# A transformer block on one core: narrow P blocks summed and masked on VectorE, row maxima turned by a DMA, variances from squares on ScalarE

## The reference

```python
mask = tril(ones((T, T))) * (arange(T) % 4 != 3)     # causal, and every fourth key is never seen
q, k, v = heads(x @ Wq + bq), heads(x @ Wk + bk), heads(x @ Wv + bv)
att = softmax(where(mask == 0, -inf, q @ k.T / sqrt(32)))
attention(x) = concat(att @ v) @ Wp + bp
idx = argmax(log_softmax(logits) + gumbel(u))
ffn(x) = x @ W[idx] + b[idx]
x = x + layernorm(attention(layernorm(x)))
x = x + layernorm(ffn(layernorm(x)))
```

## Time and profile before

| | |
|---|---|
| median of the runs | 2315.77 us |
| span of the profiled execution, first to last instruction (the page has no other time for it) | 2314.4 us |
| TensorE busy | 2226.8 us, 96% |
| VectorE busy | 1712.2 us, 74% |
| GpSimd busy | 1703.5 us, 74% |
| ScalarE busy | 1558.7 us, 67% |
| time of the busiest DMA queue's packets, as a share of 16 engines' span | 23.5% |

### The profile page before, as it was taken

How to read it: one execution, slowest core, us unless ns; L and a number is a source line. 1 busy time by engine, 2 the same in 40 slices (tenths; PEclk the granted TensorE clock), 3 DMA queues, 4 the chain that set the end, 5 groups by cost and what they waited for, 6 DMA issues and landing times.

```text
span 2314.4 us, 42414 instructions
## 1 busy us (share of the span) xinstructions
PE 2226.8 (96%) x14484; PEld 932.2 (40%) x14484; DVE 1712.2 (74%) x4758; ACT 1558.7 (67%) x2822; POOL 1703.5 (74%) x1563
## 2 busy tenths in 40 slices
PE   4899999999999999999999999999999999999997
PEld 2444433433444443343344444343344444334322
DVE  7978776876477878687368878778728787768876
ACT  7657667677755767667864766767776576675673
POOL 3248699789735879978962769988983486997852
PEclk9999999999999999999999999999999999999998
DMA  7213122112233213112132413111124231211101
GB/s 214 69 35 89 36 56 64 36 29 82 55 93 75 59 41 70 39 35 59 48 92 59 100 31 80 45 34 43 45 60 103 68 78 34 60 46 49 27 1 37
DMA packets 222818, 137.42 MB, mean 59 GB/s; under 512 B 145194, under 2 KB 195082, under 8 KB 222602
## 3 DMA queue, kind: packets, MB, share of 16 engines
q1 hardware_dynamic: 222310, 134.65, 23.5%
q10 hardware_dynamic: 292, 0.07, 0.0%
HBM read 39.69 MB, written 16.78 MB: 24 GB/s over the span
## 4 chain that ended last, share of the span: by engine, by line
PE 74%; DVE 9%; issue 6%; POOL 5%; ACT 4%; DMA 2%; SPq 0%; POOLq 0%; ACTq 0%; DVEq 0%
PE acc L1310 13%; PE acc L1346 13%; PE acc L1330 12%; PE acc L1281 9%; PE acc L1282 9%; PE acc L1283 9%; PE acc L1361 5%; POOL P L845 3%; ACT P L960 3%; DVE MP L1065 2%; PE acc L1334 2%; DVE acc L1061 2%; DVE STA L1016 1%; PE acc L1286 1%; PE acc L1318 1%
## 5 line engine op out<-in xcount | busy, mean ns | idle before, releaser
L960 ACT ACTIVATE P<-acc,EX 128x512 f32<-128x512 f32 (+2 forms) x1920 | 1084.5, 637 | 421.8 <-PE acc L1330 204.0
L845 POOL TENSOR_TENSOR P<-P 128x512 f32<-128x512 f32 x982 | 1219.4, 1277 | 65.1 <-PE acc L1346 51.3
L1065 DVE TENSOR_REDUCE MP<-acc 128x1 f32<-128x512 f32 (+1 forms) x1088 | 718.4, 679 | 172.2 <-PE acc L1310 169.4
L1310 PE MATMUL acc<-KST,QST 96*128 96x512 f16 (+10 forms) x2112 | 596.0, 334 | 24.7 <-DVE MP L1065 8.1
L1330 PE MATMUL acc<-QST,KST 98*128 98x512 f16 (+2 forms) x1920 | 589.2, 355 | 13.5 <-ACT P L960 6.6
L1061 DVE CUSTOM_DVE_ANT_0 acc<-acc,CB 128x96 f32<-128x96 f32 (+7 forms) x1024 | 450.3, 455 | 189.0 <-PE acc L1310 186.6
L1346 PE MATMUL acc<-P,V 128*32 128x512 f32 (+2 forms) x3840 | 430.6, 545 | 1.4 <-ACT P L960 0.9
L1310 PEld LDWEIGHTS acc<-KST,QST 96*128 96x128 f16 x2112 | 192.8, 97 | 364.7 <-issue 62.6
L1330 PEld LDWEIGHTS acc<-QST,KST 98*128 98x128 f16 x1920 | 183.2, 97 | 280.5 <-ACT P L960 69.5
L824 POOL TENSOR_TENSOR RR<-RR,NHALF 128x1 f32<-128x1 f32 x256 | 140.9, 555 | 185.8 <-DVE RR L1022 105.0
L836 POOL TENSOR_TENSOR QKL<-SC,QKH 128x384 f16<-128x384 f32 (+1 forms) x128 | 134.3, 1049 | 123.5 <-ACT QKH L935 123.4
(11 more groups left out here) (152 smaller groups left out, 2506.2 us busy)
## 6 DMA issues: line engine op xcount, KB each, us to landing
QST<-QKH SPq DMA_DIRECT2D x128, 128.0 KB, 3.2
XR<-in_L_attn_x_dram SPq DMA_DIRECT2D x60, 256.0 KB, 2.9
out_dram<-XR SPq DMA_DIRECT2D x60, 256.0 KB, 2.2
KST<-QKH SPq DMA_DIRECT2D x128, 96.0 KB, 2.6
XB<-in_L_attn_x_dram SPq DMA_DIRECT2D x48, 252.0 KB
QST<-QKL SPq DMA_DIRECT2D x64, 128.0 KB, 3.3
KST<-QKL SPq DMA_DIRECT2D x64, 96.0 KB, 2.7
XB<-in_L_attn_x_dram SPq DMA_DIRECT2D x20, 256.0 KB, 3.2
```

The lines of the kernel that those rows point to most:

```text
L845: e.tensor_tensor(P[:, acc, a, :], P[:, acc, a, :], P[:, buf, a, :], ALU.add).then_inc(g_s, 1)
L960: e.activation(P[:, p_buf[u, g, sb_], a, t0:512], bank(*step)[:, t0:512], ACT.Exp, scale=EX[:, 1:2]).then_inc(a_e, 1)
L1065: e.tensor_reduce(maxima(u, g)[:, r, a, ci:ci + 1], bank(*s)[:, 0:n], AX.X, ALU.max).then_inc(v_m, 1)
L1310: i = e.matmul(bank(*s)[:, 0:n], QST[0:96, h, 128 * r:128 * r + 128], KST[0:96, h, c0:c0 + n], start=True, stop=True)
```

## The change

1. **Mask.** The matmul that adds the mask to the scores is gone. VectorE takes the minimum of P and a mask of 0 and 1e38 after the exp, one instruction for the 4 x 176 elements of a block's four heads. pv, sum and add of such a block wait for it.
2. **Narrow blocks.** In 63 of 64 windows the two narrow blocks are added to the accumulator by VectorE (four heads in one instruction) and not summed on TensorE. The accumulator's own sum now comes last. In unit j = 0 block 0, summed directly before, is the accumulator of these two adds.
3. **Pairs.** GpSimd adds two heads with one instruction.
4. **Maxima.** MHL is padded to 128 columns and turned by a transposing DMA from SyncE's queue. TensorE's four transposes and ScalarE's copy are gone; the following DMAs to QST wait for the landing.
5. **Variances.** For the norms after the two projections (k = 1 and 3) ScalarE squares the row with an accumulated sum, and one small VectorE instruction stands where BN_STATS, BN_AGGR and a tensor_scalar stood. For the first norm of all units but the first, the four powers on GpSimd are one instruction.
6. **Exp.** The scale of the exp is in a register, where it was a [128, 1] operand.
7. **Planner.** The durations are changed to fit, and with them every engine's list.

```diff
+    MASK, NARROW, SQUARE, BATCH, QUADS = True, True, True, True, 2
+    EXP = 0.833, 93
+    def narrow_added(self, u, g):
+        return self.NARROW and not (u == self.NU - 1 and g == 3)
+    def added(self, u, g):
+        j = u % self.NJ
+        whole = [s for s in range(1, 3 * j + 1) if not self.on_pe(u, g, s)]
+        return whole + [3 * j + 1, 3 * j + 2] * self.narrow_added(u, g)
+    def adders(self, u, g, sb):
+        j = u % self.NJ
+        if sb > 3 * j:
+            return [("dve", 0, 4)]
...
+        return [("gp", a, self.QUADS) for a in range(0, 4, self.QUADS)]
...
-            add("pe", s - 0.2, 300, ("shift", u, g), [("dve", "peaks", u, g)])
-            add("act", s - 0.2, 480, ("shift", u, g), [("pe", "shift", u, g)], [("MROW", ("sp", "shift", u, g))])
+            add("sp", s - 0.2, 1250, ("turn_m", u, g), [("dve", "peaks", u, g)], [("MROW", ("sp", "shift", u, g))])
...
+                if masked and self.MASK:
+                    add("dve", at, 830, ("mask", u, g, sb), exps)
+                    exps = [("dve", "mask", u, g, sb)]
...
+                    e.dma_start_transpose(MROW[:, :].rearrange("p (o n) -> p o n", o=1), MHL[:, n % 2, :]).then_inc(d_h, 16)
...
+                    e.tensor_tensor(P[:, acc, h, :], P[:, acc, h, :], P[:, buf, h, :], ALU.add).then_inc(g_s, 1)
...
+                    e.activation(VOID[:, :], bank("proj", job, 0), ACT.Square, accum_out=SQ[:, k // 2, r:r + 1]).then_inc(a_s, 1)
...
                     e.activation(P[:, p_buf[u, g, sb_], a, t0:512], bank(*step)[:, t0:512], ACT.Exp,
-                                 scale=EX[:, 1:2]).then_inc(a_e, 1)
+                                 scale=factor).then_inc(a_e, 1)
...
+                        e.scalar_tensor_tensor(out=RR[:, k, 0, r:r + 1], in0=SQ[:, k // 2, r:r + 1], scalar=1.0 / 512,
+                                               in1=EC[:, k // 2:k // 2 + 1], op0=ALU.mult, op1=ALU.add).then_inc(v_ln, 1)
...
+                elif kind == "mask":
+                    part = P[:, p_buf[u, g, sb_], :, T0[i]:T0[i] + MW]
+                    for a in range(4):
+                        dv.wait_ge(a_e, AC["exp", u, g, sb_, a])
+                    e.tensor_tensor(part, part, MASKT[i].rearrange("p (o n) -> p o n", o=1).broadcast_to([128, 4, MW]),
+                                    ALU.min).then_inc(v_k, 1)
...
+                    e.tensor_tensor(P[:, acc, h, t0:512], P[:, acc, h, t0:512], P[:, buf, h, t0:512], ALU.add).then_inc(v_s, 1)
...
-                        pe.wait_ge(d_cb, 16)
-                        i = e.matmul(bank(*s)[:, t0:t0 + MW], IDB, MASKT[dg], start=False, stop=True)
```

More of the change, by code:

```diff
@@ L21, in most_chunks, with width @@
     return max(len(chunks(384 * j + 96 * (r + 1))) for r in range(4))
[L24 to L31, removed]
+def width(j, sb):
+    return (512, 512, 344, 176)[max(sb - 3 * j + 1, 0)]
 def p_blocks(NB, NJ):
@@ L278, in attend @@
                     [] if sb else [("psO", ("dve", "out", u, g))])
-            before = []
[L280 to L284, removed]
-                add("pe", s + place / (last + 1) + 0.02, 1.65 * w + 60, ("sum", u, g, sb), done + before,
+                if sb in self.added(u, g):
+                    i = self.added(u, g).index(sb)
+                    for who, a0, n in self.adders(u, g, sb):
+                        before = [("pe", "pv", u, g, 0)]
+                        if masked and self.MASK and not j:
+                            before.append(("dve", "mask", u, g, 0))
+                        if i:
+                            was = self.added(u, g)[i - 1]
+                            before = [(self.adder_on(u, g, was, a), *self.adder(u, g, was, a)) for a in range(a0, a0 + n)]
+                        done = [("dve", "mask", u, g, sb)] if masked and self.MASK else [("act", "exp", u, g, sb, a) for a in range(a0, a0 + n)]
+                        add(who, at, 142 + 2.12 * n * w if who == "gp" else 100 + 1.04 * n * w, ("add", u, g, sb, a0), done + before)
@@ new lines, in attend @@
+            before = []
+            for sb in blocks:
+                w = 512 if sb == "acc" else width(j, sb)
+                if sb == "acc":
+                    was = self.added(u, g)[-1]
+                    done = [(self.adder_on(u, g, was, a), *self.adder(u, g, was, a)) for a in range(4)]
+                    at = 3 * j if 3 * j + 1 in blocks else last
+                else:
+                    done = [("dve", "mask", u, g, sb)] if sb >= 3 * j and self.MASK else [("act", "exp", u, g, sb, a) for a in range(4)]
+                    at = sb
+                add("pe", s + at / (last + 1) + 0.02, 1.65 * w + 60, ("sum", u, g, sb), done + before,
@@ L294, in attend @@
-            add("dve", s + 0.95, 1600, ("invert", u, g), [("pe", "sum", u, g, last)]
+            add("dve", s + 0.95, 1600, ("invert", u, g), before
                 + [("dve", "out", *divmod(s - 1, 4))] * (s > 0))
@@ L707, in valued @@
             return max(AC["evac", ("v", u, a)] for a in range(3))
-        def exped(u, g, sb_):
-            return max(AC["exp", u, g, sb_, a] for a in range(4))
         block = ctx.enter_context(nc.Block())
```

294 lines of the change are left out of this document (171 added, 123 removed).

## The result

The changed kernel takes 2492.74 us (median of 4 runs, 2483.91 to 2504.35), the kernel before 2316.39 beside it. The ratio is 1.077, 95% interval 1.073 to 1.080: slower by 7.7%. The forecast was 2237 us and faster, its range ended at 2330.

What follows compares the result with a forecast made beforehand. TensorE was taken as the bound: 2314.4 - 138 = 2176 us, plus 60 us lost with a nearly full VectorE, made 2236 us of span and a forecast of 2237 us; the 8-in-10 range was 2165 to 2330.

Steps and rivals of the forecast that it cites:

- what leaves TensorE: On TensorE: masking matmuls 59 us, transposes 20 us and narrow sums 59 us go, together 138 us.
- VectorE's own work: On VectorE: 1712 us less 140 of statistics, plus 22 of tiny steps and 310 of masks and adds, 1904 us.
- the waits: On VectorE: 318 masks and narrow adds held up by GpSimd's adds, 200 us in all, bounds 0 to 380.
- The long narrow adds: A sign on VectorE: adds of 1376 elements would take above 2 us each.
- I take two and a half times that loss, 3% of some 2000 us: 60 us: TensorE's added loss from sharing fixed lists with a nearly full VectorE: 60 us, bounds 0 to 120.
- TensorE's own 2177: The run time if TensorE kept its present idle time: 2176 us of span plus 1.4 us.
- TensorE alone: Rival, 22%: TensorE stays alone at the bound, VectorE's waits are absorbed, 2177 us.
- VectorE is the bound: Rival, 15%: with waits of 380 us VectorE has 2284 us of work, and the kernel takes 2290 us.
- The end of each window: Rival, 18%: VectorE's chain adds 5.0 us at each window's end; from 2.2 us uncovered the kernel is slower.
- SyncE's part: On SyncE's queue: transposing DMAs bring a window's maxima 2.3 us later, costed at nothing; uncovered, 147 us.
- its price by mean residual, 245 us: On VectorE: by the skill's rule alone a meeting with a GpSimd pair costs 1.1 us, the waits 245 us.

Runs made afterwards that it cites:

- e5: The changed kernel with GpSimd's adds of two heads working on 16 of 512 columns, same lists and waits: 2281.38 us, ratio 0.985.
- e7: The changed kernel with GpSimd adding one head per instruction, as before the change, lists planned anew: 2516.60 us, ratio 1.087.
- f1: The changed kernel, same lists, with 16-column one-SBUF-input maxima replacing masks and narrow adds, and the one-column step as a tensor_scalar: 2253.74 us, ratio 0.973.
- f2: The kernel before the change with GpSimd's adds working on 16 of 512 columns, same lists: 2301.98 us, ratio 0.993.
- e6: The changed kernel, same lists, with masks and narrow adds cut to 16 columns a head, still two SBUF inputs: 2354.91 us, ratio 1.017.
- e2: The changed kernel with the mask put on the scores by TensorE again, lists planned anew: 2367.00 us, ratio 1.022.
- e3: The changed kernel with the narrow blocks summed by TensorE again, the mask staying on VectorE: 2436.44 us, ratio 1.051.
- e4: The changed kernel with mask and narrow sums on TensorE again and the one-column step as a tensor_scalar: 2296.58 us, ratio 0.992; repeated, 2294.78 us, ratio 0.990.
- e9: The changed kernel with the mask's table in PSUM, seven banks for the planner, narrow sums on TensorE, one-column step as a tensor_scalar: 2340.92 us, ratio 1.011.
- e10: The same as e9, with the same lists, but the mask's table read from SBUF: 2485.76 us, ratio 1.074.
- f3: e4 with the 126 narrow adds on GpSimd, four heads to an instruction: 2273.32 us, ratio 0.981.
- e11: The changed kernel with the mask on GpSimd as a 0/1 product, narrow sums on TensorE, one-column step as a tensor_scalar: 2300.75 us, ratio 0.993.
- e1: The changed kernel with the one-column step as a tensor_scalar with one SBUF input, same lists: 2483.22 us, ratio 1.072.

## Why the prediction was wrong

**Right: what leaves TensorE, and VectorE's own work.** I had 1904 us for VectorE without meetings; e5, nearly without them, shows 1901.9. Masks were 0.84 us in the working and are 0.875 at the shortest; adds of 1376 elements were 1.52 and are 1.58 at several places of the timeline.

**Right in sum, wrong in kind: the waits.** I took 200 us, and VectorE is busy 2105.2 us, where I had 2104. But I made it 318 chances of a wait of 0.9 us, less than half of the instruction in the way, and set the upper bound at 1.2. The trace has 192 masks with a median of 1.07 us and a maximum of 7.23, and a single column that stood for 11.98. The evidence I had, one add of 1.16 us, came from a place where VectorE got its turn after one GpSimd instruction. I generalized the mean from that, and e7 shows that the length of that instruction isn't what counts. I also missed one class of meeting: the 128 one-column steps, which I priced at 0.174 us by a row of the same operation. That row had one input in PSUM; the new step has both in SBUF. By the difference to e5 the waits are 118 us at the masks (302.2 against 183.8), 67 at the one-column steps (90.6 against 23.7) and 17 at the narrow adds (192.2 against 175.1). The steps that I had priced for waits have 136 of my 200, and steps that I had given none have the rest: that 2105 met 2104 is luck. The long narrow adds took 1.74 us on the mean, where I wanted over 2 as a sign.

**The step that failed** is in the sum: "I take two and a half times that loss, 3% of some 2000 us: 60 us". What stood there was 316 us, 197 of them from the meetings (below). I had read the 3% from a stretch in which GpSimd was 93% busy, whose lateness TensorE hardly felt (2.3 us of 200). VectorE stands twice in TensorE's way: its masks and narrow adds come before pv and the sums, and its reductions empty the banks of the peaks. No other work can pass a stalled instruction, because the lists are fixed; from 604 us on one such stall held TensorE for 10.04 us. TensorE's idle time was 276 us and not 147, and 108 of the added 188 us stand before pv and the sums. And I left the clock out: 0.955 against the 0.991 of before.

Of the 316 us between TensorE's own 2177 and 2493 I had forecast 60. By the runs they are:

| | us | what it holds |
|---|---|---|
| my 2176 + 1.4 | 2177 | TensorE with before's idle time, an estimate |
| f1 | 2254 | and the new places of the steps, nearly no length, no meeting |
| e5 + 15 (what short adds on GpSimd gave in f2) | 2296 | and the length, nearly no meeting |
| changed kernel | 2493 | and the meetings |

So the meetings cost some 197 us, the length 42, and 77 are for the new places together with whatever else my 2177 had wrong (TensorE's waits for rows from MROW are 16 us in f1, and 0.3 before). The split holds only in this order: with short steps, e6 against f1, nearly the same waits cost 101 us. Without meetings the change would by this estimate have brought 0.9%, and not 3.4%. That the mask is the larger part, e2 and e3 show: taking it away gives 126 us although TensorE gets some 59 us of matmuls back, for the narrow adds it is 56 us.

**The rivals.** "TensorE alone" is refuted by f1 as well. "VectorE is the bound" had the right culprit with the wrong picture: VectorE was idle for 379 us. "The end of each window", the slower one, came nearest. It named the direction, the instructions and the place where most of the added idle time stands: 69.4 + 42.1 us before pv and the sums, or 1.7 us in each of 64 windows, where it asked for 2 or more. What it had too small is the waits, 2.7 of the 5.9 us of its chain. In e5 that chain has its full length and nearly no meetings, and TensorE waits only 18.9 + 9.5 us there; the other 83 us came with the meetings. The planner, the transposing DMAs, ScalarE's squares and the pairs are cleared by e4, at least without the new steps on VectorE beside them. SyncE's part holds nearly: TensorE waited 10.6 us for rows from MROW.

The Trainium skill, "SBUF — State Buffer", section "Who interferes with whom", gave the mechanism, and e9 against e10 bears it out. I gave it no rival of its own, because its price by mean residual, 245 us, looked like mine. By its words the second waits until the first is finished; here the wait outlasted five GpSimd instructions and more.

## What to carry to other kernels

Before an elementwise step is put on VectorE, count its inputs in SBUF: with two of them beside a GpSimd that works through long runs, the price can be not the step's length but the rest of the run, and everything behind it in the list pays. One input in PSUM (e9), or the step on GpSimd itself (f3, e11), avoids the wait; each has its own price, a bank or GpSimd's time. A mean wait says little about an engine that others need every microsecond; look for the longest one and ask who is behind it. And a stall of TensorE can be charged again by its clock, as the 0.51 after the stall of 10 us was.

## What the runs showed of the hardware

- VectorE with two SBUF inputs can go without a turn through a whole run of GpSimd instructions that follow each other without a gap: 11.98 us for one column, beside adds of two heads at an unslowed 2.3 us, and five masks that end 0.75 us after such a run. Yet VectorE's adds of 512 columns in the earlier trace rows, 0.64 us alone, take 1.16 beside fourteen GpSimd adds that also follow each other without a gap, so there VectorE gets its turn. What decides it stays open; it wasn't tried by itself.
- With one of the two inputs in PSUM the spread is gone: 871 to 890 ns in 192 minima.
- A tensor_scalar on one column with a per-partition addend isn't held off: 196 to 217 ns in the 128 of e1.
- The exp with its scale in a register takes 603 ns on 512 columns where it took 694 with a [128, 1] operand, and 321 against 412 on 176: 91 ns less at either width.
